# Attention over head pairs on one Trainium2 core: another order inside a pair, and a shorter tail of the softmax sums

## The reference

```python
q = l2norm(to_heads(layer_norm(latents) @ Wq)) * q_scale        # 2 x 8 heads x 1024 x 64
k, v = to_heads(concat([layer_norm(x), layer_norm(latents)]) @ Wkv)
k = l2norm(k) * k_scale                                         # 64 + 1024 keys
sim = einsum("bhid,bhjd->bhij", q, k) * 8.0
sim = where(full_mask, sim, -max)
attn = softmax(sim)
out = layer_norm(einsum("bhij,bhjd->bhid", attn, v) @ Wo)
x = x + out
x = x + ffn(layernorm(x))          # shared expert + top 2 of 16
```

## Time and profile before

| | us |
|---|---|
| median of three runs | 852.02 (850.69 to 852.81) |
| the profiled execution, device time | 855.23 |
| its span, first to last instruction | 853.5 |
| PE busy in the span | 812.2 (95%) |
| DVE busy | 485.0 (57%) |
| ACT busy | 341.1 (40%) |
| POOL busy | 327.1 (38%) |

### The profile page before, as it was taken

How to read it: one execution, slowest core, us unless ns; L and a number is a source line. 1 busy time by engine, 2 the same in 40 slices (tenths; PEclk the granted TensorE clock), 3 DMA queues, 4 the chain that set the end, 5 groups by cost and what they waited for, 6 DMA issues and landing times.

```text
span 853.5 us, 12969 instructions
## 1 busy us (share of the span) xinstructions
PE 812.2 (95%) x4354; PEld 495.1 (58%) x4355; DVE 485.0 (57%) x905; ACT 341.1 (40%) x652; POOL 327.1 (38%) x252
## 2 busy tenths in 40 slices
PE   8999988999999999999999999999869999999987
PEld 5444344555455454555454557655536999999544
DVE  4887767866766767676772576655012333333334
ACT  3555363555656565655555311121001333333100
POOL 3000053465666656565648643204720000000463
PEclk9999999999999999999999999999969999999998
DMA  3106500000000000000020020962410222232243
GB/s 112 38 26 208 193 1 1 14 13 13 13 14 14 13 2 14 14 13 13 14 75 13 25 61 26 292 215 92 167 62 6 88 92 92 89 95 74 83 139 92
DMA packets 54116, 55.98 MB, mean 66 GB/s; under 512 B 10666, under 2 KB 49204, under 8 KB 54068
## 3 DMA queue, kind: packets, MB, share of 16 engines
q1 hardware_dynamic: 50980, 46.96, 17.7%
q0 software_dynamic: 3072, 8.39, 3.0%
q10 hardware_dynamic: 16, 0.00, 0.0%
HBM read 36.60 MB, written 18.67 MB: 65 GB/s over the span
## 4 chain that ended last, share of the span: by engine, by line
PE 84%; ACT 4%; another core or an unknown queue 3%; DVE 3%; issue 3%; POOL 2%; DVEq 1%; POOLq 0%; ACTq 0%
PE bank L910 14%; PE bank L1058 12%; PE bank L884 11%; PE bank L1121 10%; PE bank L758 9%; PE bank L1073 6%; PE bank L838 5%; PE bank L1130 5%; PE bank L893 3%; ACT prob L1234 3%; PE bank L964 2%; PE bank L822 2%; PE bank L919 2%; PE bank L1111 1%
## 5 line engine op out<-in xcount | busy, mean ns | idle before, releaser
L1234 ACT ACTIVATE prob<-bank,zero 128x512 f32<-128x512 f32 x256 | 158.7, 691 | 104.2 <-PE bank L893 103.7
L1442 DVE TENSOR_REDUCE mx<-bank 128x1 f32<-128x512 f32 x256 | 164.3, 685 | 55.7 <-PE bank L838 55.3
L678 POOL TENSOR_TENSOR acc<-acc,prob 128x1024 f32<-128x1024 f32 x64 | 152.1, 2377 | 26.3 <-ACT prob L1234 19.1
L910 PE MATMUL bank<-prob,vn 128*64 128x512 f32 x576 | 134.2, 601 | 0.6 <-DVE on L1507 0.6
L1058 PE MATMUL bank<-xfT,w12s 128*128 128x512 f32 x256 | 119.9, 610 | 11.3 <-issue 9.4
L720 POOL DMA_INDIRECT slot_result<-slot_results,posi x32 | 30.5, 953 | 188.2 <-DMA slot_results<-yo 169.5
L1121 PE MATMUL bank<-xsT,w_slot 128*128 128x128 f32 x752 | 91.9, 275 | 1.0 <-ACT xsT L1323 1.0
L1121 PEld LDWEIGHTS bank<-xsT,w_slot 128*128 128x128 f32 x752 | 89.2, 191 | 6.0 <-ACT xsT L1323 1.6
L1058 PEld LDWEIGHTS bank<-xfT,w12s 128*128 128x128 f32 x256 | 49.7, 196 | 64.3 <-issue 60.8
L684 POOL TENSOR_TENSOR acc<-acc,tail 128x1024 f32<-128x1024 f32 x16 | 38.1, 2382 | 111.1 <-DVE tail L1490 111.1
L1313 ACT ACTIVATE hidden_units<-bank 128x512 f32<-128x512 f32 x32 | 18.9, 597 | 152.4 <-PE bank L1058 114.3
(11 more groups left out here) (171 smaller groups left out, 1103.6 us busy)
## 6 DMA issues: line engine op xcount, KB each, us to landing
w12r<-in_L_ffn_routed_w SPq DMA_DIRECT2D x32, 256.0 KB
slot_rows<-zrow SPq DMA_DIRECT2D x47, 128.0 KB, 1.9
xsl<-slot_rows SPq DMA_DIRECT2D x47, 128.0 KB
slot_results<-yo SPq DMA_DIRECT2D x47, 128.0 KB, 1.7
w3r<-in_L_ffn_routed_w SPq DMA_DIRECT2D x16, 256.0 KB
rec<-row_sum_reciprocals SPq DMA_DIRECT2D x28, 128.0 KB, 2.9
xin<-in_x SPq DMA_DIRECT2D x16, 128.0 KB, 2.0
w12s<-in_L_ffn_shared_w SPq DMA_DIRECT2D x2, 1024.0 KB, 6.6
```

Source lines behind the costliest of these rows:

```text
L678: g.tensor_tensor(acc[:, m % 2, :, :], acc[:, m % 2, :, :], prob[:, (n + kt) % PROBS, :, :], ALU.add).then_inc(summed, 1)
L910: last = mm_(bank[O_BANK][rows, :], vn[:, kt, b, (2 * j + h) * DH:(2 * j + h + 1) * DH], prob[:, n % PROBS, h, :], start=(kt == 0), stop=( ...
L1234: a(prob[:, n % PROBS, h, :], bank[2 * (n % 2) + h][:, :], ACT.Exp, bias=bias).then_inc(probs_ready, 1)
L1442: v.tensor_reduce(mx[:, h, t, c:c + 1], ring_bank(u)[:, :], AX.X, ALU.max).then_inc(ring_used, 1)
```

## The change

Seven edits in the attention.

1. `LAST` goes from 3 to 2. DVE's tail is one addition (tiles 7 and 8) where it was two; POOL adds tile 6 as well (`ADDS` 7 for 6), one addition more for each of the 16 chunks.
2. The query's right turn (`Q_RIGHT`) moves from phase 1 to the start of phase 2.
3. The query's left turn (`Q_LEFT`) moves from the start of phase 0 to between its second and third slot, in pairs 1 to 6.
4. The rounds of phases 1 to 5 are 3, 4, 3, 4, 3 where they were 3, 4, 2, 4, 4.
5. ACT copies a finished output before the sums, at the start of phases 1 and 4, where it had done so behind the first slot. The wait for the division before goes with it.
6. Chunk 14's output is copied as well, so that chunk 15's first `weigh` waits for that copy and no longer for DVE's division; that division reads `o_raw` in SBUF and no longer PSUM.
7. In pair 7, from phase 1, one of the three `weigh` goes in front of the third slot.

Pair 0 has an order of its own and gets only edits 1 and 5.

```diff
-LAST = 3
+LAST = 2
...
-    TURN_AT = {0: (K_LEFT, Q_LEFT), 1: (K_RIGHT, K_CTX, Q_RIGHT)}
-    ROUNDS = {1: ((), (0,), (1,), (2,)), 2: ((3,), (4,), (5,), (6,)), 3: ((), (), (7,), (8,)),
-              4: ((9,), (10,), (11,), (12,)), 5: ((13,), (14,), (15,), (16,))}
+    TURN_AT = {0: (K_LEFT, Q_LEFT), 1: (K_RIGHT, K_CTX), 2: (Q_RIGHT,)}
+    TURN_BETWEEN = Q_LEFT
+    ROUNDS = {1: ((), (0,), (1,), (2,)), 2: ((3,), (4,), (5,), (6,)), 3: ((), (7,), (8,), (9,)),
+              4: ((10,), (11,), (12,), (13,)), 5: ((14,), (15,), (16,), ())}
...
             if kt == 0:
-                if m == NCH - 1:
-                    pe.wait_ge(o_ready, m)
-                else:
-                    wait(pe, o_kept, m)
+                wait(pe, o_kept, m)
...
+                first = SLOTS * i + BATCH * (f - 1)
+                early = not more and f > 0
...
+                    if a == BATCH - 2:
+                        for turn in between:
+                            turn_heads(*turn)
+                        if early:
+                            weigh(first)
+                for n in range(first + early, first + BATCH):
...
         def keep_o(m):
 
             act.wait_ge(pv_done, TK * (m + 1))
+            wait(act, o_ready, m - 1)
...
-                m = 2 * i - 1 if f == 1 else 2 * i if f == PHASES + 1 and i + 1 < PAIRS else -1
+                m = 2 * i - 1 if f == 1 else 2 * i if f == PHASES + 1 else -1
                 if a_ == 0 and m >= 0:
+                    keep_o(m)
+                if a_ == 0 and 0 <= m < NCH - 2:
                     keep_sum(m)
...
-            v.tensor_tensor(tail[:, :, :], prob[:, n % PROBS, :, :], prob[:, (n + 1) % PROBS, :, :], ALU.add)
-            v.drain()
-            dve.wait_ge(probs_ready, 2 * (n + LAST))
-            v.tensor_tensor(tail[:, :, :], tail[:, :, :], prob[:, (n + 2) % PROBS, :, :], ALU.add).then_inc(tail_ready, 1)
+            v.tensor_tensor(tail[:, :, :], prob[:, n % PROBS, :, :], prob[:, (n + 1) % PROBS, :, :],
+                            ALU.add).then_inc(tail_ready, 1)
```

More of the change, by code:

```diff
@@ L972, in stage_b @@
             for f in range(CH * PHASES):
+                between = turned_between(i, f)
                 for turn in phase_turns(i, f):
-                    turn_heads(*turn)
+                    if turn not in between:
+                        turn_heads(*turn)
                 places = phase_rounds(i, f)
+                first = SLOTS * i + BATCH * (f - 1)
+                early = not more and f > 0
                 for one in places[0]:
```

17 lines of the change are left out of this document (11 added, 6 removed).

## The result

The changed kernel takes 858.94 us (858.46 to 859.52, 4 runs), the kernel before beside it 852.32 (850.69 to 852.81, 4 runs): a ratio of 1.0082, 95% interval 1.0067 to 1.0097. It is 6.6 us slower, where 2.5 was forecast, and lies beyond the range's upper end of 857.0. The profiled execution of the changed kernel took 859.23 us, its span is 857.3. One execution of the changed kernel in a later set (of six) took 925.51 us at a mean granted clock of 0.851 and is left out of every median here.

A forecast was written before the change was run, and what follows sets the result against it. PE, busy 95% of the span, was taken to bound the kernel. Six pairs + 3.2, pair 0 - 0.5 and pair 7 - 0.2 gave + 2.5 us on the median 852.02: 854.5, with 8 in 10 for 850.8 to 857.0.

The forecast's parts named there:

- Phases of the middle pairs: Pairs 1 to 6: gains of 0.42, 0.27 and 0.28 against 1.50 lost in phase 2, + 0.53 us a pair.
- The chain behind the turn: Phase 2, pairs 1 to 6: the second round waits for turn, split and maxima until T + 2.82, PE idle 0.92 us.
- The upper end of phase 2: Pairs 1 to 6: the most that phase 2 was said to lengthen, 1.75 us, in a range from 1.38.
- Pair 0: Phase 3 of the first pair: without the tail's second addition DVE begins the second round's work earlier, gain 0.47 us.
- Rival A: Phase 2: DVE splits the turn before PE needs it, so the wait is hidden; - 3.5 us, 848.5; chance 0.12.
- Rival C: Last pair: chunk 14's division loses the gap to POOL's next addition, the projection is 2.4 us later; 857; chance 0.12.
- Rival B: Last pair: DVE and POOL don't start the shared expert, so the whole 3.5 us gain counts; 851.2; chance 0.14.
- Pair 7: Last pair: PE 3.5 us earlier at its projections, 0.7 left behind POOL's chain; + 0.2 us, or - 0.2 if the clock holds.
- the clock: Shared expert, behind PE's idle time of some 3 us: some slots at half clock, costing 0 to 0.9 us, taken as 0.4.
- The wait of pair 0: First pair, earlier trace: a PE wait of 1.28 us, with a shorter one behind it, was followed by slots at half clock.
- Everything behind the attention at zero: After the attention: no term of its own; the attention's difference of + 2.5 us was laid straight on the median 852.02.

The follow-up runs named there:

- tail alone: The kernel before with only LAST cut from 3 to 2 (one tail addition on DVE, one more on POOL): 835.23 us, before 833.38, ratio 1.002.

## Why the prediction was wrong

**Phases of the middle pairs: right, and to a few hundredths.**

| phase | before | after | measured | predicted |
|---|---|---|---|---|
| 0 | 8.47 | 8.04 | -0.43 | -0.42 |
| 1 | 8.19 | 7.96 | -0.23 | -0.27 |
| 2 | 7.00 | 8.54 | +1.54 | +1.50 |
| 3 | 7.58 | 7.57 | -0.01 | 0 |
| 4 | 7.06 | 7.06 | 0.00 | 0 |
| 5 | 7.81 | 7.53 | -0.28 | -0.28 |
| pair | 46.11 | 46.70 | +0.59 | +0.53 |

The table is of pair 4, which starts at 303.19 before and at 303.29 after. Six times 0.59 would be 3.5, and the six pairs differ by 3.3. The pairs don't all repeat within a tenth, as the prediction had it: pairs 2 and 6 of before take 46.4. Pair 2's 0.3 us stand at its end, where PE waits for the negated maxima of the next pair:

```profile
257.12 0.30 PE L858 MATMUL bank<-ident,zneg 128*128 128x128 f32 x1 [0.24 <-DVE zneg L1455]
```

In the changed kernel the last round is one slot earlier and this wait is gone.

The chain behind the turn, put together from the earlier trace rows with no such wait in any trace, gave the second round at T + 2.82. It stands at 322.11 - 319.29 = 2.82. The first round of phase 1 was put at T + 2.20 and stands at 313.60 - 311.33 = 2.27. Idle time at the second round was to be 0.92 and is 0.80, as PE came to it at T + 2.02 and not at T + 1.86. (The upper end of phase 2 in the pair's range, 1.75, should have been 0.58 + 1.1 = 1.68; nothing hangs on it.)

**Pair 0: right.** - 0.5 measured, - 0.47 predicted. The second round of phase 3 begins at 137.87, 1.28 behind the first, with 0.78 of idle time that is no more than what a slot would fill, where the earlier trace rows had 1.75 between the two.

**Rival A** (the turn hidden) fell with the 0.80 us, six times. **Rival C** (the division of chunk 14 loses every gap to POOL) fell as well: it took 1.75 us where it got a place between additions, and `project_o(0)` isn't late. **Rival B** (pair 7 keeps 3.5 us) fell twice: by the 3.20 us of idle time, and by edits 5 to 7 alone, which came to 1.0001 (0.999 to 1.0012).

**Pair 7: the mechanism right, the term too small.** The step said PE's phases there gain 0.58 each and 3.0 up to phase 5, that POOL's fifth addition comes behind phase 5's exponentials, that PE then idles about 3 us and half clock follows, sum - 0.2, or + 0.2 with the clock. POOL, the 3.20 us and the half clock are all there. But a `weigh` in the gap gains 0.43 a phase, not 0.58, and phase 5 begins 2.4 us earlier. POOL's five additions take 12.67 us, 2.53 each where they took 2.46, and they don't wait for the exponentials of phase 5: when the fourth is done, these have just come. The deviations start 41.74 us behind the pair's start for 40.16 before, +1.6, where the step gave about +1.1. So the second transpose is 0.2 later than before, not 0.2 earlier; and the clock, bounded at 0.9 from one row of pair 0, took 0.4 in two profiles of the changed kernel and 1.6 in the third. The wait of pair 0 that the prediction reasoned from is there in all 15 profiles and was followed by half clock in two of them. The term is + 0.5 to + 1.9 where the sum took - 0.2.

Nor was the fifth addition alone to blame, as the step had it. In the order of before it costs 2.3 us at the second transpose (tail alone), but behind the other edits only 0.3: with the turn in phase 1 the transpose comes 56.46 behind the pair's start with the short tail in the last chunk and 56.12 with the long one. What all kernels here share is the tail's own addition, 2.35 us on POOL right ahead of the deviations of row tile 1 (492.71 above). What that addition starts behind differs: in the changed kernel it is the bias, which itself waited 1.30 us for its DMA and ended after the tail was ready (490.40 + 1.22 on DVE); with the long tail POOL stands 1.16 to 2.66 us for DVE's tail, which DVE makes behind its part of row tile 0. Another place for the addition, for the bias or for DVE's tail wasn't tried, so which of them holds the second transpose isn't shown.

The lengthened division falls under the rule that the prediction quoted ("SBUF — State Buffer", section "SBUF: two separate sides", of the Trainium skill). The trace goes on agreeing, at more places: the tail's addition takes 2.24 us under POOL's additions and 1.22 without them, the division 2.23, 1.75 and 1.24 where a 128 x 512 takes 0.68 alone. None of those was shown to be on the path.

**Everything behind the attention at zero: this is the step that failed.** It was never a term at all; the difference of the attention was laid straight on the median of the whole. Where the kernel before takes 833 us that would have done: + 3.7 measured, + 3.4 in the attention, made of + 3.2 in the six pairs, - 0.5 in pair 0 and + 0.7 in pair 7. On the chip of the first result, 6.6 - 3.4 = 3.2 us lie behind it, where there are two places with waits that the traces at 833 don't have, and half clock with them. The profile of before had both, 9.6 us of waits for "issue" behind 615 and one wait of 2.8 near 833. The two profiles of the kernel before differ by 3.3 us behind the third `xf` (340.5 and 337.2); a range widened by that would have reached 860. It is not shown that the change causes the 3.2 us.

So of the 4.4 us between 854.5 and 858.94, 0.3 are the median of before, 0.1 the six pairs, 0.9 pair 7, and some 3.2 what is behind the attention. The sign, the place and the size of the main term were right. The chances gave slower 0.43, same 0.44: with pair 7 sized by the runs (+ 3.4 in all) the forecast would have been on the slower side of 0.3%, and that without what came behind.

## What to carry to other kernels

Before an operation is moved in a ring of buffers, write out the chain that frees its buffer (here turn, ACT's copy, DVE's split, first maxima, release: 2.82 us) and see that as much other work of the producer stands behind it at the new place. Closing gaps on the busiest engine pays only up to the point where it meets another engine's chain; there the small gaps come back as one long gap, with half the clock behind it. And before the difference of one stage is laid on the whole, look whether the other stages repeat from one profile to the next: one stage with waits that nothing in the profile explains is worth a wider range.

## What the runs showed of the hardware that was not expected

- 1.9 us or more of idle time on PE, in the midst of work at 2.4 GHz, was followed by a stretch at 1.2 GHz in all eleven profiles that had it ahead of the second transpose, 3.4 us long or twice that: the shared expert's 16 matmuls took 8.56 to 8.80 us with the one and 9.35 to 10.01 with the other, and 7.17 where the idle time had been filled with four matmuls. With 0.2 us idle (the kernel before, and the one with the turn moved alone) there was none. Which of the two follows doesn't go with the idle time: the longer behind 1.89, 1.93, 2.27, 2.48, 3.20 and 3.21 us, the shorter behind 1.90, 1.92, 3.19, 3.20 and 3.27. Nor does it always follow: near the end of the span waits of 2.56, 2.63 and 3.06 us had none behind them, and 2.83, 3.13, 3.17 and 3.23 had.
- The same kernel takes 833 us on some chips and 852 on others. 14 to 17 us of the difference lie between the third `xf` and the first slot, where PE waits for "issue" up to 2.42 us at a time; the rest comes behind it, with one wait of 2.6 to 3.2 us.
- DVE's work with two inputs in SBUF isn't starved by a queue of POOL additions with 0.1 us between them: it got the place behind the addition under way each time. The divisions took 1.75 and 2.23 us, 1.1 and 1.6 more than the 0.68 of one alone, and one addition takes 2.38.
